# A two-part transformer block on one core: the split of the next batch's shift moved ahead of the token store, its load ahead of the stack, row and key loads, and the zero rows taken out

## The chip, the cores and the metric

The kernel runs on one core of one Trainium2 chip. The metric is the time of one execution on the device in microseconds (us). The kernel before was executed three times on the chip: 641.44, 649.53 and 644.13 us, median 644.13 us. Lower is better. Differences of under 2% count as no difference that can be told.

## The reference: what is computed

The inputs are `x` and `ctx_2048`, 16 batches of 128 rows by 512 features in fp32, two gates, and a mixture of 8 experts (`wg` 512x8, `W` 8x512x512, `b` 8x512).

```python
x = x + jnp.tanh(g_xattn[0]) * _L0_xattn_ref(_layernorm(x), ctx_2048, ctx_2048)
x = x + jnp.tanh(g_ffn[0]) * _L0_ffn_ref(_layernorm(x), wg, W, b)
# _L0_xattn_ref(q, k, v): 8 heads of 16 features over the 128 rows
qk = jnp.einsum('bdm,bdn->bmn', qh, kh) * scale      # 512 x 512 a head
ret = jnp.einsum('bmn,bcn->bcm', softmax(qk), vh)
# _L0_ffn_ref(x, wg, W, b): the one expert with the largest logit
idx = jnp.argmax(softmax(xt @ wg)); out = gate * (W[idx] @ xt + b[idx])
```

Here the 512 features of a row are the positions that attend to each other, and a head is 16 of the 128 rows. So a batch has 8 score matrices of 512x512, each with a contraction of only 16. The softmax subtracts the maximum of each of the 512 positions of a head, which the kernel calls the shift.

## The kernel before, in words

**Numbers in three parts.** To get fp32 accuracy from bf16 matmuls, GpSimd and ScalarE split q and k of a batch into three bf16 parts each (high, middle, low) and GpSimd stores them in DRAM (`parts_dram`, 768 KB a batch, L471). SyncE then loads them back stacked on the partitions: six terms of 16 rows are 96 rows (`KS`). `load_stack(B, g)` loads one half (g is 0 or 1, four heads each) of one batch: for q three copies of the high part, two of the middle and one of the low part (L329, each a broadcast of one source), for k the matching parts (L333), 192, 128 and 64 KB for each of the two. Rows 96 to 127 of a stack are padding: the three rows 96 to 98 (`KS` to `KS + NP`) of the k stack hold ones, those of the q stack hold the three bf16 parts of the shift, the others are zero. There are two stacks for even and odd batches (`B.p`).

**Two passes over the scores.** First the maxima: 32 matmuls of a batch write 128x512 scores into `ps_ring` (`scores_for_max`, L1099), two buffers, and VectorE takes the negated maximum of each (L756). After four of the eight heads PE transposes the maxima (L1105), VectorE copies them into `shift` (`take_maxima`), GpSimd splits them into three bf16 rows (`split_maxima`, L495 to L503) and SyncE copies these into the q stack (`load_shift`, L343, three small DMAs). Then the scores again, transposed and with the shift added by the matmul (`scores`, L1115, contraction over all 128 rows), exponentials on ScalarE (L672), and the product with the values and with ones (L1130). Because the maxima matmul also contracts over 128 rows, the shift rows of the q stack must be zero while it runs: `load_stack` ends with a seventh DMA that copies three rows of zeros there (L337).

**Rounds.** The kernel is written as 16 rounds of `emit(B, ...)` on each engine. Rounds 0 and 1 and 12 to 15 are straight code, rounds 2 to 11 are a hardware loop of two rounds in the body. In round B, PE works on the scores of batch B and between them on the maxima of batch B+1; the routing of batch B-2 and the split of q and k of batch B+3 lie in it too. The order on every engine is the order of the code, and engines meet at semaphores. On PE a round begins with the wait for `shift_in[0]` and `scores(B, 0, 0)`; directly behind stands the first maxima matmul of batch B+1, which waits for `stack_in[B.p][0]`, that is for all DMAs of `load_stack(B+1, 0)`.

**SyncE in round B**, in order: one slice of the expert weights, `load_shift(B, 1)`, the record of batch B-2, the residual input of batch B-1 (`load_residual`), `load_stack(B+2, 0)`, `load_rows_keys(B+4)` (x and k, 256 KB each), `load_shift(B+1, 0)`, `load_stack(B+2, 1)` and `load_values(B+2)`. `load_stack(B+2, 0)` waits until half of the scores of round B are done, `load_shift(B+1, 0)` until GpSimd's split of that shift (`shift_ready`), `load_stack(B+2, 1)` until all scores of round B are done. All these DMAs are on one queue.

**GpSimd in round B** ends the LayerNorm of x after attention (`rstd2`, L435 to L441), stores the token numbers of batch B-2 by an indirect DMA (`store_tokens`, L517 to L525), splits the shift (`split_maxima(B+1, 0)`), and makes and stores the low parts of batch B+3 (`lows`, L469 and L471).

After round 15 come 23 slots of the experts, to which the change does nothing.

Of the kernel before, what the change touches and what calls it, by code (L numbers as in the profile page):

```python
# [112 lines left out]
def build(nc, x_rows, x_perm, k_perm, v_t, w_t, wg_t, bias, g_attn, g_ffn, out):  # L113
    ctx = ExitStack()
    with ctx:
# [25 lines left out]
        slot_iota = sb("slot_iota", [128, 1])  # L141
        zeros = sb("zeros", [NP, NJ * DM], BF16)
        none_i = sb("none_i", [128, 128], I32)
# [122 lines left out]

        STACK_CONSTS, VALUE_CONSTS = 3, 4
        DVE_CONSTS = 17
        POOL_CONSTS = 13
# [28 lines left out]
        def _(sp):  # L298
# [20 lines left out]
            def load_stack(B, g):  # L319
# [12 lines left out]
                for first, n in ((0, 3), (3, 2), (5, 1)):  # L332
                    sp.dma_start(k_stack[first * DH:(first + n) * DH, B.p, g].rearrange("p j m -> p (j m)"),  # L333
                                 mine[1, g, 0:n].rearrange("t c m -> (t c) m")).then_inc(stack_in[B.p][g], 16)
                if B.known(0) and g == 0:
                    sp.wait_ge(pads_in, 16)
                sp.dma_start(q_stack[KS:KS + NP, B.p, g].rearrange("p j m -> p (j m)"),  # L337
                             zeros[:]).then_inc(stack_in[B.p][g], 16)

# [38 lines left out]
            def emit(B, prev, prev2, nxt, prep):  # L378
                load_weights(B)
                load_shift(B, 1)  # L380
                if B.known(NB - 1):
                    sp.wait_ge(scores_ready, 2 * STEPS * (NB - 1))
                    sp.dma_start(bias_sb.rearrange("p e n -> p (e n)"), bias.partition_broadcast(128)).then_inc(bias_in, 16)
                if prev2:
                    store_record(B.plus(-2))
                stack = not isinstance(B.b, int) or B.b + 2 < NB
                load_residual(B)
                if stack:
                    load_stack(B.plus(2), 0)
                if not isinstance(B.b, int) or B.b + 4 < NB:  # L390
                    load_rows_keys(B.plus(4))
                if nxt:
                    load_shift(B.plus(1), 0)
                if stack:
                    load_stack(B.plus(2), 1)
                    load_values(B.plus(2))
# [7 lines left out]
        def _(pool):  # L404
# [165 lines left out]
            def emit(B, prev, prev2, nxt, prep):  # L570
# [10 lines left out]
                if prev:  # L581
                    rstd2(B.plus(-1))
                if prev2 and not B.known(NB - 1):
                    store_tokens(B.plus(-2))
                if B.known(NB - 1):
# [3 lines left out]
                    for r in range(NREC):  # L589
                        gather(r, r)  # L590
                if nxt:
                    split_maxima(B.plus(1), 0)
                if prep:
# [134 lines left out]
        def _(dve):  # L728
# [3 lines left out]
                           lambda: nc.vector.memset(stacks[KS:KS + NP, 0, 1].rearrange("p g j m -> p (g j m)"), 1.0),  # L732
                           lambda: nc.vector.memset(zeros[:], 0.0),
                           lambda: nc.vector.memset(v_ones[:].rearrange("p a c g j d -> p (a c g j d)"), 1.0)]
# [356 lines left out]
        def _(pe):  # L1091
            def scores_for_max(B, u, n, k, chunks=range(NC)):

                g, j = divmod(k, NJ)
                if j == 0 and 0 in chunks:
                    pe.wait_ge(stack_in[B.p][g], B.i * (16 * 7) + 16 * 7)
                for c in chunks:
                    wait(pe, ring_free, u.free(n + c))
                    nc.tensor.matmul(ps_ring[:, u.slot(n + c)], q_stack[0:KA, B.p, g, j, c * 128:(c + 1) * 128],  # L1099
                                     k_stack[0:KA, B.p, g, j], start=True, stop=True).then_inc(ring_full, 1)  # L1100

# [6 lines left out]
            def scores(B, k, jp):  # L1108

                g, c = divmod(k, NC)  # L1110
                if c == 0 and jp == 0:
                    pe.wait_ge(shift_in[g], B.b * 48 + 48)
                wait(pe, exp_done, B.b * (2 * STEPS) + (2 * k + jp - 1))
                for j in (2 * jp, 2 * jp + 1):
# [201 lines left out]
```

## Time and profile before

| | us |
|---|---|
| median of 3 executions | 644.13 (641.44 to 649.53) |
| span of the profiled execution | 645.9 |
| first scores matmul of round 0 | at 57.91 |
| first scores matmul of round 2 | at 116.02 |
| first scores matmul of round 12 | at 413.33 |

Of the profiled execution the span is all that is reported; what lies around it is not given apart. The span is 1.8 us over the median of the three executions.

PE is busy 83% of the span, VectorE 73%, ScalarE 55%, GpSimd 50%. SyncE's DMA queue moves 62 MB, GpSimd's 25 MB. Times in a row of the trace are microseconds from the start of the span; a row of the chain of waits names what the end of the program waited for in turn; in a row of a stretch the numbers behind each engine are its busy time. In the text, S is the start of a round, the moment at which PE begins `scores(B, 0, 0)`: 326.07 for the round shown, 355.30 for the next.

### The profile page before, as it was taken

To read this page: it belongs to the slowest core of one execution; us is meant where nothing else is said; L and a number is where in the kernel's file an instruction comes from. 1 tells how busy PE (TensorE), PEld (TensorE's weight loads), DVE (VectorE), ACT (ScalarE), POOL (GpSimd) and SP (SyncE) were. 2 spreads that over 40 slices of the span, in tenths; PEclk is the share of its full clock that TensorE was granted. 3 is DMA by queue.
4 is the path that set the end of the run, shared out by engine and by line. 5 is a ranking of instruction groups with operands and counts; after the bars stand their busy time and mean duration, and the time that the engine had idled before them with its cause. 6 is when DMAs were issued, how large, how long until landed. Compare 5 with 4: busy or idle time off the path is not lost.

```text
span 645.9 us, 10904 instructions
## 1 busy us (share of the span) xinstructions
PE 533.8 (83%) x2584; PEld 179.0 (28%) x2585; DVE 469.3 (73%) x1017; ACT 352.5 (55%) x457; POOL 325.5 (50%) x574
## 2 busy tenths in 40 slices
PE   0077989798978989999988899889999776889994
PEld 0011222222222323323222322323233133444441
DVE  5387888696878979898988989798987636323332
ACT  2112867575766677686766677686666822111110
POOL 5431536282737556474736557474434436343541
PEclk9999999798999999999999999999999978999998
DMA  4734445364647574846657575835462645543320
GB/s 131 189 105 154 116 134 148 102 151 130 131 150 179 148 171 127 195 136 159 141 142 180 145 167 146 184 113 148 104 141 42 179 132 177 117 144 96 102 79 5
DMA packets 35290, 87.80 MB, mean 136 GB/s; under 512 B 10281, under 2 KB 10430, under 8 KB 35104
## 3 DMA queue, kind: packets, MB, share of 16 engines
q1 hardware_dynamic: 26208, 62.27, 39.3%
q0 software_dynamic: 9056, 25.23, 12.1%
q8 instruction: 11, 0.18, 0.1%
q14 instruction: 15, 0.12, 0.1%
HBM read 64.56 MB, written 27.11 MB: 142 GB/s over the span
## 4 chain that ended last, share of the span: by engine, by line
PE 31%; DMA 18%; DVE 17%; issue 11%; POOL 9%; SPq 3%; ACT 1%; POOLq 0%; DVEq 0%
DMA stacks<-shift_parts 13%; DVE neg_max L756 11%; PE ps_scores L1238 10%; PE ps_pv L1130 7%; PE ps_ring L1099 6%; PE ps_scores L1115 4%; DMA table_dram<-token_i,dest_i 2%; SPq L343 2%; DMA prep<-recs_dram,token_cols 2%; PE ps_pv L1147 2%; POOL table_dram L523 2%; POOL prep L463 2%; DVE den L794 1%; ACT probs L672 1%; PE ps_scores L1225 1%
## 5 line engine op out<-in xcount | busy, mean ns | idle before, releaser
L756 DVE TENSOR_REDUCE neg_max<-ps_ring 128x1 f32<-128x512 f32 x512 | 335.4, 680 | 76.1 <-PE ps_ring L1099 74.1
L672 ACT ACTIVATE probs<-ps_scores 128x1024 f32<-128x1024 f32 x256 | 249.2, 1022 | 112.0 <-PE ps_scores L1115 110.8
L1099 PE MATMUL ps_ring<-stacks 128*128 128x512 bf16 x512 | 201.0, 403 | 55.3 <-DMA stacks<-zeros 30.7
L1115 PE MATMUL ps_scores<-stacks 128*128 128x512 bf16 x512 | 156.1, 388 | 20.2 <-DMA stacks<-shift_parts 19.2
L1130 PE MATMUL ps_pv<-probs,v_ones 128*32 128x512 f32 x1024 | 138.2, 612 | 0.0
L1099 PEld LDWEIGHTS ps_ring<-stacks 128*128 128x128 bf16 x512 | 49.6, 97 | 240.6 <-DVE neg_max L756 191.0
L1238 PE MATMUL ps_scores<-w_sb,probs 128*128 x184 | 87.2, 619 | 3.3 <-DVE v_ones L927 1.3
L435 POOL TENSOR_SCALAR rs<-mv 128x1 f32<-128x1 f32 x32 | 6.1, 189 | 131.7 <-DVE mv L772 89.4
L1115 PEld LDWEIGHTS ps_scores<-stacks 128*128 128x128 bf16 x512 | 48.1, 101 | 65.4 <-issue 25.2
L710 ACT COPY probs<-ps_scores 128x512 f32<-128x512 f32 x23 | 13.4, 587 | 82.2 <-PE ps_scores L1225 82.2
L927 DVE TENSOR_TENSOR v_ones<-ps_scores,stacks 128x512 f32<-128x512 f32 x23 | 15.9, 692 | 57.6 <-PE ps_scores L1238 55.2
L1238 PEld LDWEIGHTS ps_scores<-w_sb,probs 128*128 128x128 f32 x184 | 34.4, 197 | 40.5 <-issue 40.4
L556 POOL DMA_INDIRECT out<-stacks,token_cols x23 | 23.5, 1023 | 43.3 <-DVE stacks L931 40.7
L463 POOL TENSOR_TENSOR prep<-prep 128x512 f32<-128x512 f32 x32 | 36.4, 1156 | 3.8 <-ACT prep L644 3.8
L469 POOL TENSOR_TENSOR prep<-prep 128x512 bf16<-128x512 f32 x32 | 36.2, 1149 | 0.0
L649 ACT CAST prep<-prep 128x512 bf16<-128x512 f32 x32 | 19.7, 618 | 25.2 <-POOL prep L463 25.2
L644 ACT CAST prep<-prep 128x512 bf16<-128x512 f32 x32 | 18.4, 619 | 24.0 <-DMA prep<-k_perm 17.5
L782 DVE STREAM_TRANSPOSE den_turned<-ps_pv 128x512 f32<-128x512 f32 x32 | 22.4, 699 | 11.0 <-PE ps_pv L1130 8.0
L484 POOL TENSOR_TENSOR num<-num,den 128x512 f32<-128x512 f32 x15 | 19.0, 1270 | 22.0 <-DVE den L794 19.5
L534 POOL COPY recip_turned<-recip 128x256 f32<-128x256 f32 x32 | 12.6, 393 | 33.8 <-DVE recip L788 33.8
L1130 PEld LDWEIGHTS ps_pv<-probs,v_ones 128*32 128x32 f32 x1024 | 20.3, 108 | 32.7 <-issue 19.7
L523 POOL DMA_INDIRECT table_dram<-token_i,dest_i x16 | 18.1, 1129 | 12.7 <-DVE neg_max L756 10.3
(138 smaller groups left out, 481.1 us busy)
## 6 DMA issues: line engine op xcount, KB each, us to landing
parts_dram<-prep POOLq DMA_DIRECT2D x16, 768.0 KB, 7.1
stacks<-parts_dram SPq DMA_DIRECT2D x64, 192.0 KB
recs_dram<-rec SPq DMA_DIRECT2D x16, 514.0 KB, 3.9
stacks<-parts_dram SPq DMA_DIRECT2D x64, 128.0 KB
w_sb<-w_t SPq DMA_DIRECT2D x16, 512.0 KB, 9.4
prep<-x_perm SPq DMA_DIRECT2D x16, 256.0 KB, 5.2
prep<-k_perm SPq DMA_DIRECT2D x16, 256.0 KB, 8.3
v_in<-v_t SPq DMA_DIRECT2D x16, 256.0 KB, 8.9
```

The lines of the kernel that those rows point to most:

```text
L463: nc.gpsimd.tensor_tensor(resid[:, s], src[:], parts[:, s, 0], ALU.subtract).then_inc(rest_ready, 1)
L469: nc.gpsimd.tensor_tensor(parts[:, s, 2], resid[:, s], parts[:, s, 1], ALU.subtract).then_inc(low_ready, 1)
L523: pool.indirect_dma_start(table_dram, bass.IndirectOffsetOnAxis(ap=dest_i[:, 0:1], axis=0), token_i[:], None).then_inc(table_out, 16)
L556: pool.indirect_dma_start(out, bass.IndirectOffsetOnAxis(ap=token_cols[:, s:s + 1], axis=0), y_out[r], None, bounds_check=NT - 1, oob_is_e ...
L649: nc.scalar.copy(parts[:, s, 1], resid[:, s]).then_inc(mid_cast, 1)
L672: nc.scalar.activation(probs[:, k % 2, 2 * jp:2 * jp + 2], ps_scores[:, jp], ACT.Exp).then_inc(exp_done, 1)
L756: nc.vector.tensor_reduce(neg_max[:, g, j, c:c + 1], ps_ring[:, u.slot(n)], AX.X, ALU.max, negate=True).then_inc(ring_free, 1)
L782: nc.vector.transpose(den_turned[:, g], ps_pv[:, g]).then_inc((low_turned, high_turned)[g], 1)
L1099: nc.tensor.matmul(ps_ring[:, u.slot(n + c)], q_stack[0:KA, B.p, g, j, c * 128:(c + 1) * 128], k_stack[0:KA, B.p, g, j], start=True, stop= ...
L1115: last = nc.tensor.matmul(ps_scores[:, jp, j % 2], k_stack[0:KA, B.p, g, j, c * 128:(c + 1) * 128], q_stack[0:KA, B.p, g, j], start=True, ...
L1130: last = nc.tensor.matmul(ps_pv[32 * j:32 * j + 32, g], v_ones[:, B.p, c, g, j], probs[:, k % 2, j], start=c == 0, stop=c == NC - 1)
L1238: last = nc.tensor.matmul(ps_y[:, r % 2], f_xt[:, r % 2, c], w_sb[:, c, bass.ds(e, 1)].rearrange("p o n -> p (o n)"), start=c == 0, stop=c ...
```

## The change

It has three parts. On GpSimd `split_maxima(B+1, 0)` moves ahead of `store_tokens(B-2)`. On SyncE `load_shift(B+1, 0)` moves ahead of `load_stack(B+2, 0)` and `load_rows_keys(B+4)`. And the maxima matmul contracts over 96 rows (`KS`) in place of 128, so that the DMA of the zero rows, its source buffer and that buffer's memset go; `load_stack` now issues six DMAs, and PE's wait counts six. The wait for the padding of the odd stacks (`pads_in`), which SyncE held ahead of the first zeros DMA, is now on PE ahead of the scores of batches 0 and 1.

```diff
@@ load_stack (SyncE) @@
                     sp.dma_start(k_stack[first * DH:(first + n) * DH, B.p, g].rearrange("p j m -> p (j m)"),
                                  mine[1, g, 0:n].rearrange("t c m -> (t c) m")).then_inc(stack_in[B.p][g], 16)
-                if B.known(0) and g == 0:
-                    sp.wait_ge(pads_in, 16)
-                sp.dma_start(q_stack[KS:KS + NP, B.p, g].rearrange("p j m -> p (j m)"),
-                             zeros[:]).then_inc(stack_in[B.p][g], 16)
@@ emit (SyncE) @@
                 load_residual(B)
+                if nxt:
+                    load_shift(B.plus(1), 0)
                 if stack:
                     load_stack(B.plus(2), 0)
                 if not isinstance(B.b, int) or B.b + 4 < NB:
                     load_rows_keys(B.plus(4))
-                if nxt:
-                    load_shift(B.plus(1), 0)
@@ emit (GpSimd) @@
                 if prev:
                     rstd2(B.plus(-1))
+                if nxt:
+                    split_maxima(B.plus(1), 0)
                 if prev2 and not B.known(NB - 1):
                     store_tokens(B.plus(-2))
...
-                if nxt:
-                    split_maxima(B.plus(1), 0)
                 if prep:
                     lows(B.plus(3))
@@ constants (VectorE) @@
-                           lambda: nc.vector.memset(zeros[:], 0.0),
@@ scores_for_max, scores (PE) @@
-                    pe.wait_ge(stack_in[B.p][g], B.i * (16 * 7) + 16 * 7)
+                    pe.wait_ge(stack_in[B.p][g], B.i * (16 * 6) + 16 * 6)
...
-                    nc.tensor.matmul(ps_ring[:, u.slot(n + c)], q_stack[0:KA, B.p, g, j, c * 128:(c + 1) * 128],
-                                     k_stack[0:KA, B.p, g, j], start=True, stop=True).then_inc(ring_full, 1)
+                    nc.tensor.matmul(ps_ring[:, u.slot(n + c)], q_stack[0:KS, B.p, g, j, c * 128:(c + 1) * 128],
+                                     k_stack[0:KS, B.p, g, j], start=True, stop=True).then_inc(ring_full, 1)
...
                     pe.wait_ge(shift_in[g], B.b * 48 + 48)
+                    if B.known(0) or B.known(1):
+                        pe.wait_ge(pads_in, 16)
```

**SyncE, in the middle of a round of the loop, before** (the program of the queue; `stacks<-shift_parts` is the shift load, `stacks<-parts_dram` the stack load, ISA and REGISTER_ALU rows are waits and register work):

```order
L317 DMA x_in<-x_rows 128x512
...
L329 DMA stacks<-parts_dram 48x1x2048
L329 ISA
L329 DMA stacks<-parts_dram 32x1x2048
...
L337 DMA stacks<-zeros 3x2048
L80 ISA
L303 ISA
L303 DMA prep<-x_perm 128x512
L304 DMA prep<-k_perm 128x512
L341 ISA
L343 DMA stacks<-shift_parts 1x16x128 x3
```

and now:

```order
L316 DMA x_in<-x_rows 128x512
L336 ISA
L338 DMA stacks<-shift_parts 1x16x128 x3
L80 ISA
L80 REGISTER_ALU
L328 ISA
L328 DMA stacks<-parts_dram 48x1x2048
...
L332 DMA stacks<-parts_dram 16x2048
L80 ISA
L302 ISA
L302 DMA prep<-x_perm 128x512
L303 DMA prep<-k_perm 128x512
```

The shift load with its wait stands directly behind the residual input, and the stack, row and key loads stand behind it; the zeros DMA is gone.

**GpSimd, between the statistics of LayerNorm 2 and the low parts, before:**

```order
L441 TENSOR_TENSOR rs<-rs,minus 128x1
L80 REGISTER_ALU
L517 CAST dest_i<-dest_f 128x1
L518 CAST token_i<-token_f 128x1
L74 REGISTER_ALU
L523 DMA table_dram<-token_i,dest_i 16384x1
L525 TENSOR_SCALAR token_f<-token_f 128x1
L493 REGISTER_ALU
L495 CAST shift_parts<-shift 16x128
...
L503 TENSOR_TENSOR shift_parts<-shift_rest,shift_parts 16x128
```

and now:

```order
L436 TENSOR_TENSOR rs<-rs,minus 128x1
L488 REGISTER_ALU
L490 CAST shift_parts<-shift 16x128
...
L498 TENSOR_TENSOR shift_parts<-shift_rest,shift_parts 16x128
L80 REGISTER_ALU
L512 CAST dest_i<-dest_f 128x1
L513 CAST token_i<-token_f 128x1
L74 REGISTER_ALU
L518 DMA table_dram<-token_i,dest_i 16384x1
```

The four instructions of the split have changed places with the token store; their number is the same.

## Rows read from the trace of the kernel before

**Rows 1.** The waits, longest first: engine, line, releaser, us in total, times, longest.

```profile
PE ps_scores L1115 <- DMA stacks<-shift_parts: 19.2, 12, 3.1
```

**Rows 2.** Stretches: us, busy us of each engine, PEclk, DMA share, GB/s.

```profile
57.91:85.80 27.89, 25.96 (x122) 7.20 (x123) 22.52 (x38) 19.16 (x22) 10.41 (x20) 1.00 0.37 104
85.80:116.02 30.22, 25.18 (x134) 7.22 (x135) 24.17 (x43) 20.70 (x25) 15.54 (x28) 0.98 0.60 149
116.02:413.33 297.31, 264.14 (x1440) 83.23 (x1441) 253.88 (x560) 209.61 (x270) 173.02 (x320) 0.98 0.60 150
413.33:441.97 28.64, 26.01 (x145) 8.26 (x145) 25.46 (x55) 20.58 (x27) 17.20 (x32) 1.00 0.47 140
441.97:469.41 27.44, 25.88 (x145) 8.16 (x144) 24.45 (x54) 18.53 (x23) 10.76 (x23) 1.00 0.51 117
116.02:146.10 30.08, 28.42 (x144) 8.71 (x144) 24.70 (x55) 20.66 (x27) 17.35 (x32) 0.90 0.52 125
148.96:177.94 28.98, 27.36 (x144) 8.50 (x144) 24.68 (x55) 20.64 (x27) 17.30 (x32) 0.94 0.55 124
326.07:354.09 28.02, 26.04 (x144) 8.24 (x144) 24.69 (x55) 20.54 (x27) 17.28 (x32) 1.00 0.62 157
```

**Rows 3.** The chain of waits at the end of the round shown: start, us, what.

```profile
348.79 6.39 DMA stacks<-shift_parts
```

**Rows 4.** PE by time: start, us, instruction, count, idle before it and releaser.

```profile
341.71 0.59 PE L1115 MATMUL ps_scores<-stacks 128*128 128x512 bf16 x2
...
355.30 0.60 PE L1115 MATMUL ps_scores<-stacks 128*128 128x512 bf16 x2 [1.21 <-DMA stacks<-shift_parts]
355.73 0.38 PE L1099 MATMUL ps_ring<-stacks 128*128 128x512 bf16 x1
```

**Rows 5.** SyncE's queue by time, in the same round.

```profile
339.87 0.35 SPq L317 DMA_DIRECT2D x_in<-x_rows  x1
340.68 2.40 SPq L329 DMA_DIRECT2D stacks<-parts_dram  x3
343.29 1.25 SPq L333 DMA_DIRECT2D stacks<-parts_dram  x3
344.60 0.73 SPq L337 DMA_DIRECT2D stacks<-zeros  x1
...
346.13 0.37 SPq L304 DMA_DIRECT2D prep<-k_perm  x1
347.53 1.85 SPq L343 DMA_DIRECT2D stacks<-shift_parts  x3
351.75 2.59 SPq L329 DMA_DIRECT2D stacks<-parts_dram  x3
```

**Rows 6.** GpSimd by time, in the same round, and the same line in round 0.

```profile
75.19 0.42 POOL L503 TENSOR_TENSOR shift_parts<-shift_rest,shift_parts 16x128 bf16<-16x128 f32 x1
...
343.14 0.19 POOL L441 TENSOR_TENSOR rs<-rs,minus 128x1 f32<-128x1 f32 x1
...
345.81 0.28 POOL L495 CAST shift_parts<-shift 16x128 bf16<-16x128 f32 x1
...
347.08 0.42 POOL L503 TENSOR_TENSOR shift_parts<-shift_rest,shift_parts 16x128 bf16<-16x128 f32 x1
```

**Rows 7.** DMA issues from 340 to 360 us: KB each, us from issue to landing.

```profile
x_in<-x_rows SPq DMA_DIRECT2D x1, 256.0 KB, 3.3
prep<-k_perm SPq DMA_DIRECT2D x1, 256.0 KB, 8.5
```

**Rows 8.** Stretches of one us, columns as in rows 2.

```profile
351.00:352.00 1.00, 0.86 (x5) 0.24 (x3) 1.00 (x3) 0.99 (x2) 1.00 (x3) 1.00 0.19 65
352.00:353.00 1.00, 1.00 (x9) 0.16 (x8) 1.00 (x3) 0.95 (x2) 0.31 (x2) 1.00 1.02 365
```

**Rows 9.** The start: SyncE's first stack load, and PE's first maxima matmul.

```profile
16.71 2.42 SPq L329 DMA_DIRECT2D stacks<-parts_dram  x3
...
30.69 1.01 PE L1099 MATMUL ps_ring<-stacks 128*128 128x512 bf16 x2 [30.69 <-DMA stacks<-zeros]
```

More of the change, by code:

```diff
@@ L141, in build @@
         slot_iota = sb("slot_iota", [128, 1])
-        zeros = sb("zeros", [NP, NJ * DM], BF16)
         none_i = sb("none_i", [128, 128], I32)
@@ L265, in build @@
         y_stored = [sem(f"y_stored{r}") for r in range(NREC)]
-        STACK_CONSTS, VALUE_CONSTS = 3, 4
-        DVE_CONSTS = 17
+        STACK_CONSTS, VALUE_CONSTS = 2, 3
+        DVE_CONSTS = 16
         POOL_CONSTS = 13
```

## The prediction, as it stood before the result

> **What bounds the kernel now.** I read the waits first, then stretches of rounds, the chain of waits, and the queues of the round that starts at S = 326.07.
>
> The waits say what the change aims at: PE stands 19.2 us in 12 waits, at most 3.1 us each, at the first scores of a round, for the shift load [rows 1]. The stretches put it in scale. Ten rounds from 116.02 to 413.33 take 297.3 us, 29.7 each, while an undisturbed one is through its work in 28.0 us and waits for the rest [rows 2]. PE is busy 26.0 of those 28.0 us, VectorE 24.7. So nothing shorter than 28.0 us a round can come of this change, about 17 us in all. Rounds 2 and 3, which follow waits of about 3 us, take 30.1 and 29.0 us of work at granted clocks of 0.90 and 0.94, a mix of the 2.4 and the 1.2 GHz level [rows 2].
>
> The chain ends a round with the last of the three shift DMAs, issued at 348.79 and landed 6.4 us later, at 355.2; PE's scores begin at 355.30 and the first maxima matmul of the batch after next follows 0.43 us behind [rows 3, 4]. The reader should look at who is ahead of that DMA: on the same queue the stack load from 340.68, the zeros, and x and k; GpSimd is done with the split only at 347.5, because the token store lies before it [rows 5, 6].
>
> The decisive question is what becomes of the stack load, which the change puts behind the shift. PE needs it 0.43 us after the shift, at the same place of its program. Its own landing isn't shown, so I read it from its neighbours. k, issued at 346.13 behind it, takes 8.5 us and lands at 354.6, while x_in with little ahead of it takes 3.3 us for the same 256 KB [rows 7]. And from 351 to 352 the 16 DMA engines are busy for a share of 0.19, about three engines, although k and the shift are still out [rows 8]. A few engines have a tail of stack packets that the others have finished.
>
> **The change part by part.**
>
> *Split ahead of the token store.* GpSimd ends the LayerNorm statistics at 343.33 (343.14 + 0.19) and the split takes 1.69 us (345.81 to 347.50) [rows 6]. It will be done at 345.0, that is S + 18.95, 2.5 us earlier. The token store slips by 1.7 us; its result is wanted a round later, and the low parts behind both end where they did. Cost nothing.
>
> *Shift load first.* SyncE has issued x_in at 340.2 and now waits for the split until 345.0. The three shift DMAs take 1.85 us to issue [rows 5]. Last issue S + 20.2; with 3.3 us, as for x_in [rows 7], or even with 6.4 us [rows 3], they land by S + 26.6, before PE is ready at S + 28.0. The wait of rows 1 goes: up to -17 us in the loop by itself.
>
> *The stack load behind it.* It was issued from 340.68, S + 14.6; now from 345.0 + 0.05 + 1.85 + 0.3 (SyncE's steps between loads in the loop) = 347.2, S + 21.15: 6.5 us later. How long from the first issue to the landing?
> - At least 7.2 us: its issues take 3.9 us (340.68 to 344.54) [rows 5], and the last then needs the 3.3 us of x_in [rows 7].
> - At most 14.0 us: the first stack load of the kernel is issued from 16.71, and PE starts on it at 30.69 [rows 9], with 512 KB of padding ahead of it.
> - Nearest is k behind it: landed 354.6, so 13.9 us after 340.68 with the 512 KB of x and k in it. At the 365 GB/s of a full stretch [rows 8] these take 1.4 us; that leaves 12.5 for the stack load.
> I take 13.0: the parts store of GpSimd, 768 KB from about 352 on [rows 8], lay only at the end of the stack load before and now falls inside it. The range and the rivals keep 7.2 and 14.0.
>
> The Trainium skill (DMA: Bandwidth & Descriptors, Rules for kernel authors) says that a leading broadcast of c copies confines a DMA to at most c engines. By it the three-copy and two-copy loads of q put 16 packets of 4 KB each on the same first engines, and the tail is what it should be; the share of 0.19 in rows 8 agrees. Had all 16 engines shared the load, the sum would be that of the first rival below.
>
> *The next round.* The stack lands at S + 21.15 + 13.0 = S + 34.15. The maxima matmul starts 0.14 later, and a round counts from 0.43 before it: a round lasts 33.9 us in place of 29.7. PE stands about 5.6 us in it.
>
> *What is behind the stack load.* The key load is issued at about S + 25.5 in place of S + 20.1 [rows 5] and lands behind the stack, about 1.5 us into the next round's maxima; it is wanted 3 us in. The second half of the stack (351.75, S + 25.7) was waiting for the scores and moves by a few tenths. No cost.
>
> *Zero rows.* Each of 28 stack loads in the rounds loses an issue of 0.73 us [rows 5], on a queue whose engine waits. At the start four of them lie on the way to the first shift: gain between 0 and 2.9 us; I take 0.8, for they are 12 KB against 768. The matmul with 96 rows has no row in this trace; its columns stay 512, and between nothing and a quarter of its 0.38 us [rows 4] I take nothing, since VectorE's maxima stand behind each. The memset of the zeros lies before the first parts have landed.
>
> *The clock.* Waits of about 3 us were followed by 2.05 and 0.96 us of extra work time in rounds 2 and 3 (30.08 and 28.98 against 28.02) [rows 2], and by none in the round after. Mean 1.0 us. The new standstill is longer and comes every round: 1.0 us for each of 13 rounds is 13; between 0 and 2.05 each.
>
> **The sum**, without the clock:
>
> | rounds | before [rows 2] | now | difference |
> |---|---|---|---|
> | 0 (split done at 75.61, S + 17.7 [rows 6]) | 27.9 | 17.7 + 1.95 + 13.0 - 0.29 = 32.4 | +4.5 |
> | 1, as 0 | 30.2 | 32.4 | +2.2 |
> | 2 to 11 | 297.3 | 10 x 33.9 = 339 | +41.7 |
> | 12, straight code | 28.6 | 33.6 | +5.0 |
> | 13, without the parts store | 27.4 | 33.0 | +5.6 |
>
> That is +59.0, less 0.8 at the start, plus 13 for the clock: +71.2. On the span of 645.9 us this is 717; the median of the runs is 1.8 us lower, so **715 us**. The ends: a landing of 12.5 us and no cost of the clock give 14 x 0.5 less, +51, 695 us; 14.0 us and 2.05 us a round give +14 + 13.7, +99, 743 us.
>
> **The rivals.**
> - *The stack load spreads over all engines and is in time* (faster). Landing 7.2 us after the first issue, at S + 28.35, just when the maxima matmul wants it (28.0 + 0.43). Then 17 us of waits go, 3 us of slow clock behind them and 0.8 at the start: 623 us. For it: 365 GB/s are reached at times [rows 8], and 768 KB at that rate take 2.1 us. Against it: k's 8.5 us and the start [rows 7, 9]. It decides from a landing under 29.73 - 21.15 - 0.14 + 0.43 = 8.9 us, where the round is as long as now. The Trainium skill (DMA: Bandwidth & Descriptors, Bandwidth) has 1 MB in 6.15 us over 128 partitions, of which an estimate for 768 KB would be 4.6 us, on this side too. Chance 0.09.
> - *In between*: 9 to 12 us, if traffic of x_in, records and parts had stretched the tail before. At 10.5 a round is 31.4: (10.5 - 13.0) x 14 = -35, some 680 us with part of the clock. Chance 0.13, of it 0.05 within 2%.
> - *The other shift becomes late as well* (slower still). Its three DMAs stand behind the second stack half. With the first landed 0.3 us into the round, x and k 1.4, the second half some 10 and values and weights 2, it lands at S + 13.5 to 14; PE wants it at 341.71, S + 15.6 [rows 4]. Slack 2 us. If the tails are longer by 3 us, each round gains one more: 13 to 30 us, 745 us. Chance 0.08.
> - That the change doesn't do what it says is excluded by the order of the two queues.
>
> My forecast has 0.70. The range takes in its ends and most of the case in between: 674 to 743 us. Within 2% is 631 to 657 us, about what a measurement of this kernel can tell from no change. Faster 0.08, same 0.06, slower 0.86.
>
> **What the profile after would show.** The waits of PE for the shift gone, and in their place, at the first maxima matmul of a round, one of about 5 us for the stack load in each of rounds 1 to 14. SyncE's stack load first issued at S + 21. The shift's three DMAs landing in 2 to 4 us. Rounds of 33 to 36 us, with a granted clock under 1 in the stretch behind most of these waits. The split done at S + 19, the token store behind it. I am wrong if the stack load lands within 9 us of its first issue; then the round falls to its 28.0 us.

## The result: 755 us, slower by 17.5%

The changed kernel takes **755.1 us** (median of 4 runs, 753.6 to 758.7), the kernel before beside it 646.1. The ratio is **1.175** (95% interval 1.167 to 1.183); ratios in this document compare executions in the chip's faster state alone, so they aren't the quotients of the medians. I had forecast 715 us in a range of 674 to 743: the sign and the order of waits came out, the size didn't, and the time lies 12 us over the range.

The page of the kernel after: span, busy us of PE and VectorE, then the granted clock of TensorE and the DMA share in 40 equal slices.

```profile
span 753.2 us, 10831 instructions
PE 561.6 (75%) x2544; PEld 187.2 (25%) x2585; DVE 469.1 (62%) x1016; ACT 353.9 (47%) x457; POOL 325.0 (43%) x574
PEclk9999897789787788988888899999998998899998
DMA  4642617161718162626161627261514255454230
```

The DMA engines now work in bursts, and the clock falls in the same rhythm. Its mean is 0.892, where it was 0.975.

The waits after: engine, line, releaser, us in total, times, longest.

```profile
PE ps_ring L1093 <- DMA stacks<-parts_dram: 132.8, 15, 30.9
PEld ps_ring L1093 <- DMA stacks<-parts_dram: 28.0, 4, 8.3
```

The wait for the shift [rows 1] is gone from this list. The wait for the stack load took its place: 15 waits of the matmuls, of which the longest is the start of the kernel, as in [rows 9], and 4 of the weight loads. They are those of the first maxima matmul of a round. PE by time shows three of them, with the idle time in brackets:

```profile
355.17 0.60 PE L1093 MATMUL ps_ring<-stacks 96*128 96x512 bf16 x1 [6.64 <-DMA stacks<-parts_dram]
...
392.98 0.61 PE L1093 MATMUL ps_ring<-stacks 96*128 96x512 bf16 x1 [6.25 <-DMA stacks<-parts_dram]
...
433.51 0.60 PE L1093 MATMUL ps_ring<-stacks 96*128 96x512 bf16 x1 [9.11 <-DMA stacks<-parts_dram]
```

From 91.13 to 579.12 there are 14 such rows, each of 5.2 to 9.5 us, and a round between two of them lasts 37.5 us.

GpSimd's rows of the round that starts at 355.17, the counterpart of [rows 6], and SyncE's queue, that of [rows 5]:

```profile
375.47 0.28 POOL L490 CAST shift_parts<-shift 16x128 bf16<-16x128 f32 x1
...
376.74 0.42 POOL L498 TENSOR_TENSOR shift_parts<-shift_rest,shift_parts 16x128 bf16<-16x128 f32 x1
...
378.23 1.11 POOL L518 DMA_INDIRECT table_dram<-token_i,dest_i  x1 [0.81 <-POOL token_i L513]
...
382.56 0.94 POOL L466 DMA_DIRECT2D parts_dram<-prep  x1 [0.68 <-POOL prep L464]
```

```profile
377.19 1.79 SPq L338 DMA_DIRECT2D stacks<-shift_parts  x3
379.46 2.28 SPq L328 DMA_DIRECT2D stacks<-parts_dram  x3
...
383.97 0.38 SPq L303 DMA_DIRECT2D prep<-k_perm  x1
384.70 2.17 SPq L328 DMA_DIRECT2D stacks<-parts_dram  x3
```

Everything that has to come first stands in this order: split, shift, stack. The second half of the stack is issued 5.2 us behind the first half; it was 11.1 us behind [rows 5]. The token store, which stood 3.7 us behind the first issue of the stack load, now stands 1.2 us ahead of it, and the parts store stands 3.1 us behind it in place of 9.7. Before, in the round of [rows 5] with its stack load at 340.68, the two stood here:

```profile
344.42 1.12 POOL L523 DMA_INDIRECT table_dram<-token_i,dest_i  x1 [0.79 <-DVE neg_max L756]
...
350.42 0.95 POOL L471 DMA_DIRECT2D parts_dram<-prep  x1 [0.68 <-POOL prep L469]
```

The chain of waits hangs on the stack: the load's last DMA, issued at 382.82, takes 10.0 us, and PE goes on 0.12 us later.

```profile
382.82 10.04 DMA stacks<-parts_dram
```

Landings in the window of 376 to 392 us (columns of [rows 7], the last being us from issue to landing):

```profile
parts_dram<-prep POOLq DMA_DIRECT2D x1, 768.0 KB, 9.9
...
prep<-k_perm SPq DMA_DIRECT2D x1, 256.0 KB, 10.7
stacks<-shift_parts SPq DMA_DIRECT2D x3, 4.0 KB, 1.7
```

Stretches, columns as in [rows 2]: ten rounds, one round, and pieces of that round from its beginning.

```profile
127.18:507.75 380.57, 288.44 (x1416) 91.42 (x1442) 254.31 (x560) 210.93 (x270) 172.58 (x320) 0.85 0.43 118
355.17:392.98 37.81, 30.04 (x142) 9.67 (x145) 25.44 (x56) 21.15 (x27) 17.27 (x32) 0.82 0.36 106
351.00:355.00 4.00, 0.00 (x0) 0.00 (x0) 0.00 (x0) 0.00 (x0) 0.00 (x0) 0.54 1.06 282
355.00:361.00 6.00, 5.83 (x21) 2.32 (x22) 3.63 (x8) 1.02 (x1) 0.00 (x0) 0.50 0.27 103
361.00:365.00 4.00, 4.00 (x14) 1.48 (x18) 2.22 (x7) 2.23 (x3) 2.85 (x9) 0.50 0.09 34
365.00:369.00 4.00, 3.80 (x26) 0.98 (x20) 3.63 (x11) 3.43 (x7) 1.27 (x1) 1.00 0.02 3
```

Ten rounds take 380.6 us against 297.3, with the same numbers of VectorE and GpSimd instructions. In one round PE is busy 30.0 us where an undisturbed one of [rows 2] had 26.0. Behind the wait of 6.64 us PE works at 1.2 GHz (0.50) for ten microseconds, from 355 to 365, before the clock is back. And in the four us before PE goes on, from 351 to 355, the DMA share is 1.06: the last packets of the stack load don't go out on otherwise idle engines here, as they did before [rows 8], but beside other loads. All but 0.05 of that share are packets of SyncE's queue; those of GpSimd's, the parts store, take a share of 0.3 to 0.7 from 347 to 351.

### The profile page after: what moved, and what is told of

It reads as the page before. It is cut to its first block, busy times and chain, and to the rows that moved or that the text cites. A ratio compares the mean times of both kernels' runs of the same rounds, so it can differ in the third digit from the quotient of the medians.

```text
span 753.2 us, 10831 instructions
## 1 busy us (share of the span) xinstructions
PE 561.6 (75%) x2544; PEld 187.2 (25%) x2585; DVE 469.1 (62%) x1016; ACT 353.9 (47%) x457; POOL 325.0 (43%) x574
## 4 chain that ended last, share of the span: by engine, by line
DMA 30%; PE 28%; DVE 13%; issue 10%; SPq 10%; POOL 7%; DVEq 0%; POOLq 0%; ACT 0%
DMA stacks<-parts_dram 21%; DVE neg_max L750 8%; PE ps_ring L1093 7%; PE ps_pv L1126 7%; PE ps_scores L1234 6%; SPq L328 4%; PE ps_scores L1111 4%; SPq L338 3%; DMA prep<-recs_dram,token_cols 3%; DMA prep<-k_perm 2%; SPq L332 2%; PE ps_pv L1143 2%; DMA table_dram<-token_i,dest_i 2%; POOL prep L458 2%; DVE den L788 1%
## 5 line engine op out<-in xcount | busy, mean ns | idle before, releaser
L1093 PE MATMUL ps_ring<-stacks 96*128 96x512 bf16 x512 | 213.0, 430 | 153.4 <-DMA stacks<-parts_dram 132.8
L1126 PE MATMUL ps_pv<-probs,v_ones 128*32 128x512 f32 x1024 | 149.1, 657 | 0.0
L1093 PEld LDWEIGHTS ps_ring<-stacks 96*128 96x128 bf16 x512 | 50.2, 98 | 354.2 <-DVE neg_max L750 195.9
L1234 PE MATMUL ps_scores<-w_sb,probs 128*128 x184 | 85.3, 607 | 2.5 <-issue 1.4
L1111 PEld LDWEIGHTS ps_scores<-stacks 128*128 128x128 bf16 x512 | 51.7, 106 | 47.5 <-issue 9.8
L705 ACT COPY probs<-ps_scores 128x512 f32<-128x512 f32 x23 | 13.4, 586 | 79.5 <-PE ps_scores L1221 79.5
L551 POOL DMA_INDIRECT out<-stacks,token_cols x23 | 23.5, 1023 | 40.1 <-DVE stacks L925 37.6
L464 POOL TENSOR_TENSOR prep<-prep 128x512 bf16<-128x512 f32 x32 | 36.2, 1149 | 0.0
L479 POOL TENSOR_TENSOR num<-num,den 128x512 f32<-128x512 f32 x15 | 19.0, 1269 | 27.6 <-DVE den L788 25.0
L776 DVE STREAM_TRANSPOSE den_turned<-ps_pv 128x512 f32<-128x512 f32 x32 | 22.3, 698 | 11.0 <-PE ps_pv L1126 8.0
## 6 DMA issues: line engine op xcount, KB each, us to landing
w_sb<-w_t SPq DMA_DIRECT2D x16, 512.0 KB, 13.1
```

Of the source, the lines that this page charges most:

```text
L464: nc.gpsimd.tensor_tensor(parts[:, s, 2], resid[:, s], parts[:, s, 1], ALU.subtract).then_inc(low_ready, 1)
L551: pool.indirect_dma_start(out, bass.IndirectOffsetOnAxis(ap=token_cols[:, s:s + 1], axis=0), y_out[r], None, bounds_check=NT - 1, oob_is_e ...
L776: nc.vector.transpose(den_turned[:, g], ps_pv[:, g]).then_inc((low_turned, high_turned)[g], 1)
L1093: nc.tensor.matmul(ps_ring[:, u.slot(n + c)], q_stack[0:KS, B.p, g, j, c * 128:(c + 1) * 128], k_stack[0:KS, B.p, g, j], start=True, stop= ...
L1111: last = nc.tensor.matmul(ps_scores[:, jp, j % 2], k_stack[0:KA, B.p, g, j, c * 128:(c + 1) * 128], q_stack[0:KA, B.p, g, j], start=True, ...
L1126: last = nc.tensor.matmul(ps_pv[32 * j:32 * j + 32, g], v_ones[:, B.p, c, g, j], probs[:, k % 2, j], start=c == 0, stop=c == NC - 1)
```

## The experiments

All ratios are to the kernel before, run on the same chip, with their 95% interval. S is the start of a round, as before. "Landing" is the time from the first issue of a round's stack load to the last increment of its semaphore, read from the trace as a mean over rounds. It is 14.6 us in the kernel after (12.9 to 16.7, 14 loads) and was 12.8 before (12.0 to 14.1). The length of a round is the mean of rounds 2 to 11, from first scores to first scores: 29.7 us before, 38.0 after.

### The parts alone

**e1: the change with SyncE's old order.** What is left is the split ahead of the token store, and no zeros.

```diff
                 load_residual(B)
-                if nxt:
-                    load_shift(B.plus(1), 0)
                 if stack:
                     load_stack(B.plus(2), 0)
                 if not isinstance(B.b, int) or B.b + 4 < NB:
                     load_rows_keys(B.plus(4))
+                if nxt:
+                    load_shift(B.plus(1), 0)
```

> The changed kernel with SyncE's order of before (stack, rows and keys, then the shift); the split ahead of the token store and the missing zero rows stay. Theory A (a stack load leaves a tail on a few DMA engines, and the loss is that it starts 6.5 us later): the stack is issued at S + 14.6 again and is in time; the shift is ready earlier but lands behind the same tail, at about S + 28.6 in place of 29.1. Time 635 to 646 us, within 2% of before. Theory B (the loss is in the 96-row matmul or in the late token store): 750 us, as the changed kernel. Theory C (the shift's landing follows its issue, not the tail): 625 us.

Measured 669.7 us, 1.027 (1.020 to 1.035). My theory missed: the order accounts for most of the loss, but the rest should have been a small gain and is a loss. The waits of e1:

```profile
PE ps_scores L1111 <- DMA stacks<-shift_parts: 39.2, 12, 5.9
```

It is twice that of [rows 1], although the split is done earlier. The stack landed 14.1 us after its issue here, and the shift stands behind it: its last DMA lands 10.5 us after its issue (mean of ten rounds), where it took 6.5 before. So it comes at S + 32.7 in place of S + 29.6, although it is issued 0.8 us earlier, and a round takes 32.9 us.

**e2: SyncE's new order alone.**

```diff
                 load_residual(B)
+                if nxt:
+                    load_shift(B.plus(1), 0)
                 if stack:
...
-                if nxt:
-                    load_shift(B.plus(1), 0)
```

> The kernel before with SyncE's order alone changed (shift, stack, rows and keys); the split stays behind the token store, the zero rows stay. Theory A: the stack waits for a split that is ready 2.5 us later than in the changed kernel, in rounds 2 to 13: 755 + 12 x 2.5 = 785 us. Theory B (the other two parts carry the loss): 650 us. If only the combination costs: under 755 us.

Measured 783.8 us, 1.214 (1.204 to 1.224), as worked out beforehand: the split is 2.5 us later than in the kernel after, and a round takes 39.6 us. A wait of its PE by time:

```profile
370.50 0.61 PE L1099 MATMUL ps_ring<-stacks 128*128 128x512 bf16 x1 [10.58 <-DMA stacks<-zeros]
```

So the load order costs the bulk of the loss, 137 us alone and 85 us with the earlier split (e1 to the kernel after).

**e6: only the zero rows gone.** The stack load has six DMAs and the maxima matmuls 96 rows.

```diff
-                sp.dma_start(q_stack[KS:KS + NP, B.p, g].rearrange("p j m -> p (j m)"),
-                             zeros[:]).then_inc(stack_in[B.p][g], 16)
...
-                    nc.tensor.matmul(ps_ring[:, u.slot(n + c)], q_stack[0:KA, B.p, g, j, c * 128:(c + 1) * 128],
+                    nc.tensor.matmul(ps_ring[:, u.slot(n + c)], q_stack[0:KS, B.p, g, j, c * 128:(c + 1) * 128],
```

> The kernel before with the third part of the change alone: 96 rows in the maxima matmul and no zeros DMA; split and shift load where they were. It takes apart the 22 us that e1 is slower than before, against its expectation. Theory E (the loss of e1 comes of GpSimd's new order: the token store now runs into the tail of the stack load and the parts store): 636 to 646 us, as before or a little better. Theory F (it comes of the missing zeros or of the 96-row matmul): 665 us or more.

Measured 651.9 us, 1.008 (1.005 to 1.011), over the 636 to 646 that I expected: nothing gained, a trace lost, and not the loss that would have explained e1. The group of its maxima matmuls:

```profile
L1093 PE MATMUL ps_ring<-stacks 96*128 96x512 bf16 x512 | 200.7, 403 | 55.7 <-DMA stacks<-parts_dram 31.0 <-DVE neg_max L750 12.8 <-ACT probs L667 1.8
```

512 matmuls of 96 rows take 403 ns in the mean. The kernel before has 403 ns for 128 rows as well:

```profile
L1099 PE MATMUL ps_ring<-stacks 128*128 128x512 bf16 x512 | 201.0, 403 | 55.3 <-DMA stacks<-zeros 30.7 <-DVE neg_max L756 12.9 <-ACT probs L672 1.6
```

**e11: only the split moved ahead of the token store.** The mirror of e2, on GpSimd.

```diff
                     rstd2(B.plus(-1))
+                if nxt:
+                    split_maxima(B.plus(1), 0)
                 if prev2 and not B.known(NB - 1):
                     store_tokens(B.plus(-2))
...
-                if nxt:
-                    split_maxima(B.plus(1), 0)
```

> The kernel before with the second part of the change alone: the split of the shift ahead of the token store on GpSimd; SyncE's order and the zeros as before. e6 (zeros alone) was 0.8% slower than before, e1 (zeros and split) 2.7%. Theory E (the moved token store carries e1's loss): 660 to 675 us, although the split is ready 2.5 us earlier. Rival (the two parts only cost together): 640 to 648 us.

Measured 674.4 us, 1.041 (1.031 to 1.051), inside what was expected. This is e1's loss by itself: its wait for the shift is 43.4 us in 12, at most 6.5, and the stack lands after 14.4 us (up to 18.2). With the old order the earlier split can gain little anyway: SyncE reaches the shift at 346.13 + 0.37 = 346.5, 1.0 us before the split's end at 347.5 [rows 5, 6]. What it moves is the token store, from 3.7 to 5.3 us behind the first issue of the stack load. The shift's last DMA lands 9.8 us after its issue, nearly as late as in e1.

### The landing of the stack

**e3: the kernel after with the q loads cut into DMAs of 16 rows**, nine per stack load instead of six, none with a broadcast of copies in front.

```diff
-                    sp.dma_start(q_stack[first * DH:(first + n) * DH, B.p, g].rearrange("p j m -> p (j m)"),
-                                 mine[0, g, t].unsqueeze(0).to_broadcast([n, DH, NJ * DM])
-                                 ).then_inc(stack_in[B.p][g], 16)
+                    for i in range(first, first + n):
+                        sp.dma_start(q_stack[i * DH:(i + 1) * DH, B.p, g].rearrange("p j m -> p (j m)"),
+                                     mine[0, g, t]).then_inc(stack_in[B.p][g], 16)
...
-                    pe.wait_ge(stack_in[B.p][g], B.i * (16 * 6) + 16 * 6)
+                    pe.wait_ge(stack_in[B.p][g], B.i * (16 * 9) + 16 * 9)
```

> The changed kernel with the three-copy and the two-copy load of q written as three and two loads of 16 rows each: nine DMAs of 16, 32 or 48 rows in place of six, the same bytes. Theory A: each spreads over all engines, the tail goes, the stack lands 6 to 8 us after its first issue in place of 14.6, at S + 28 to 30, and rounds take 28 to 30 us: 620 to 655 us. Theory D (the landing is long because of the total traffic, x, k, parts and the other half included, not because of a few engines): the landing stays over 12 us and the time over 730 us.

Measured 666.9 us, 1.029 (1.023 to 1.035). The mechanism holds: 88 us of the 109 go. The size is short of what I expected (620 to 655 us), since the landing fell to 9.7 us (8.2 to 12.1), and not to 6 to 8. Its waits:

```profile
PE ps_ring L1093 <- DMA stacks<-parts_dram: 57.7, 15, 24.3
```

**e4: the same loads with SyncE's old order** (e1 and e3 together).

> The q loads as in the run with nine DMAs, but SyncE's order of before (e1's kernel with nine DMAs). Theory A: stack issued early and no tail in front of the shift: it lands within 3 us of its issue, PE waits neither for the shift nor for the stack, rounds of 28.0 us, full clock: 620 to 630 us, the best so far. Theory D: as e1, 640 us.

Measured 613.9 us, 0.947 (0.942 to 0.952): better than expected, and the fastest of all. Its waits and, from a window of 300 to 330 us, the landing of two loads:

```profile
PE ps_ring L1093 <- DMA stacks<-parts_dram: 25.3, 1, 25.3
PE ps_scores L1111 <- DMA stacks<-shift_parts: 2.1, 3, 0.9
...
prep<-k_perm SPq DMA_DIRECT2D x1, 256.0 KB, 3.7
stacks<-shift_parts SPq DMA_DIRECT2D x6, 4.0 KB, 2.3
```

The stack lands after 7.2 us and k behind it after 3.7 instead of 8.5 [rows 7]. The row of the shift is the median of six DMAs; the last of three, which PE waits for, took 6.4 us before [rows 3] and takes 6.3 here (mean of ten rounds), not the 3 that I expected. With the tail, in e1, it took 10.5. Against the kernel before it is issued 1.8 us earlier (S + 21.3 against S + 23.1); so it lands at S + 27.6, is hardly waited for any more, and a round takes 28.1 us, about the length of its work. PE's first maxima matmul also comes 5.4 us earlier, since the first load at the start lands sooner, and the first scores 9.1 us earlier (48.80 against 57.91).

**e7: the kernel before with the q loads cut up**, nothing else.

> The kernel before, with nothing of the change, and the three-copy and two-copy loads of q as DMAs of 16 rows (ten DMAs a stack load in place of seven). Theory A: the tail alone was what made the shift late before; it lands within 6 us of its issue and before PE wants it, rounds of 28.0 us, and the start is shorter: 612 to 622 us, within 1% of e4, so the change's own parts give nothing on top. Rival: the change's parts are needed as well: 630 us or more.

Measured 617.4 us, 0.957 (0.953 to 0.962), as expected. The waits for the shift are down to this:

```profile
PE ps_scores L1115 <- DMA stacks<-shift_parts: 4.9, 7, 1.8
```

So most of the shift wait that the change attacks goes with the tail of the stack load alone, with the old order on both queues: the shift's last DMA lands after 5.4 us instead of 6.5, at S + 28.1 instead of S + 29.6, and a round takes 28.4 us. That is 13 us over rounds 2 to 11; another 9 of the 30 us lie at the start, where the first scores begin at 48.51. The stack lands after 9.6 us here (7.2 to 11.9), not after e4's 7.2. And the new order loses 53 us even with the short tail (e3 against e4).

Why does the tail exist? The Trainium skill (DMA: Bandwidth & Descriptors, Rules for kernel authors) says that a leading broadcast of c copies confines a DMA to at most c engines, and these runs agree: without the broadcasts the load lands after 7.2 us instead of 14.1 (e4 against e1). An estimate by that rule is that of the 192 packets of 4 KB of a stack half two engines get 39 each (16 and 16 of the broadcasts, 7 of the rest), where an even spread would give each 12. The traces here don't name the engine of a packet.

**e8: the change with the shift between the stack and rows and keys.**

```diff
                 load_residual(B)
-                if nxt:
-                    load_shift(B.plus(1), 0)
                 if stack:
                     load_stack(B.plus(2), 0)
+                if nxt:
+                    load_shift(B.plus(1), 0)
                 if not isinstance(B.b, int) or B.b + 4 < NB:
```

> The changed kernel with the shift load between the stack load and the rows and keys, six DMAs a stack load as in the change. Theory A: the stack is issued at S + 14.6 and lands in time, the shift stands behind its tail but no longer behind rows and keys, and lands about 1 us earlier than in e1: 10 to 14 us under e1's 670, 655 to 660 us. If rows and keys ahead of the shift cost nothing: 670 us.

Measured 636.7 us, 0.983 (0.976 to 0.991). I expected 655 to 660 and missed on the good side, though against the kernel before the gain is under 2%: the shift wait is 9.8 us in 8, the stack lands after 13.1 us, and a round takes 29.0 us. I had charged the shift with the whole tail in front of it. But SyncE, waiting for the split, holds x and k back as well, and these no longer join the stack on the engines. Against e1 the shift's last DMA is issued 1.9 us earlier (S + 20.4 against S + 22.3) and lands 2.1 us sooner after that (8.4 against 10.5). That the second part comes of the held x and k is argued, not shown.

**e10: the kernel after, with SyncE holding x, k and the second half until the first half has landed.**

```diff
                     load_stack(B.plus(2), 0)
+                    sp.wait_ge(stack_in[B.p][0], B.plus(2).i * (16 * 6) + 16 * 6)
```

> The changed kernel, with SyncE waiting until load_stack(B+2, 0) has landed before it issues rows, keys and the second half. The other side of e9. Theory H: the landing falls from 14.6 to about 13 us. Theory G: it stays at 14 to 15 us. In time the landing gained and the rows and keys that now come late at the next round's start may cancel: 735 to 775 us.

Measured 739.0 us (two runs), 1.139 (1.125 to 1.152). The landing is 13.4 us on the mean, and a round takes 37.0 us. Its queue and PE:

```profile
330.68 2.27 SPq L328 DMA_DIRECT2D stacks<-parts_dram  x3
333.27 1.26 SPq L332 DMA_DIRECT2D stacks<-parts_dram  x3
344.37 0.35 SPq L302 DMA_DIRECT2D prep<-x_perm  x1
```

```profile
344.21 0.61 PE L1094 MATMUL ps_ring<-stacks 96*128 96x512 bf16 x1 [6.25 <-DMA stacks<-parts_dram]
```

With nothing of SyncE's behind it the load of this round too still takes from 330.7 to 344.1, 13.4 us. The traffic behind accounts for about 1.2 of the 14.6 us. The rest is the load's own tail, the token store and the parts store. The tail can be seen in this run: from 340 to 342 and from 342 to 344 the DMA share is 0.16 and 0.08, one to three engines of 16, while PE waits for the stack.

### The clock

**e5: the kernel after, with 24 matmuls on constants between the scores and the first maxima matmul**, so that PE works where it waited.

```diff
+                    if nxt and k == 0 and B.b is not None and not B.known(0):
+                        wait(pe, ring_free, u.free(n))
+                        for _ in range(24):
+                            nc.tensor.matmul(ps_ring[:, u.slot(n)], ones_bf[:], filler[:], start=True, stop=True)
```

> The changed kernel, and in rounds 1 to 15, once PE has done the first scores and before it waits for the stack load, 24 matmuls of constants (128x128 by 128x512, bf16) into the free buffer of ps_ring, which the true matmul then overwrites: some 5 us of work inside a wait of 6 to 8 us. It leaves the waits and the loads as they are. Theory A' (of the 755 us the clock is a larger part than the 13 us of my sum: after each wait the granted clock is at the 1.2 GHz level for a while, and the next shift is issued 20.7 us after the first maxima matmul on the mean of 13 rounds, where an undisturbed round has 18.4): clock near 1.0 in the rounds, the time 20 to 32 us lower, 723 to 735 us. If the clock costs only what my sum had: 742 us. If it costs nothing: 755 us or more.

Measured 745.7 us, 1.150 (1.140 to 1.161), with runs from 738 to 758: less gained than the 20 to 32 us that I expected. The clock rose from 0.892 to 0.958. PE by time at the place:

```profile
372.51 5.34 PE L1185 MATMUL ps_ring<-filler,ones_bf 128*128 128x512 bf16 x24
378.01 0.39 PE L1095 MATMUL ps_ring<-stacks 96*128 96x512 bf16 x1 [0.16 <-DMA stacks<-parts_dram]
```

The filling takes 5.34 us, the wait behind it shrinks to 0.16, and the first maxima matmul takes 0.39 us instead of 0.60. From a landing to the next first issue it is 21.8 us instead of 22.9, and a round between two first maxima matmuls 36.2 instead of 37.5. In five rounds of the loop, this one among them, the granted clock is 1.00 between these two points, and they lie 20.9 to 21.0 us apart, where I had 20.86. The 9 us of gain are a lower bound of what the clock costs, because in seven of 13 rounds it still fell.

### The token store

**e9: the kernel after without the token store.** A plain DMA of 512 bytes to a scratch tensor stands in its place.

```diff
-                pool.indirect_dma_start(table_dram, bass.IndirectOffsetOnAxis(ap=dest_i[:, 0:1], axis=0),
-                                        token_i[:], None).then_inc(table_out, 16)
+                pool.dma_start(scratch_dram, none_i[0:1, :]).then_inc(table_out, 16)
```

> The changed kernel with the token store left out: in place of the indirect DMA of 128 four-byte writes GpSimd issues one plain DMA of 512 bytes to a scratch buffer at the same place. The routing table stays empty, so the expert stage after round 15 moves no rows, and its time isn't to be compared; the rounds are. It asks why a stack load lands 14.6 us after its first issue in the changed kernel (mean of 14) where 12.8 was read before. Theory G (the token store, issued 1.2 us ahead of the stack load, holds up all 16 DMA engines for 2 to 4 us when they next read): landings of 12.5 to 13.5 us, none over 14.5, rounds 1 to 2 us shorter than 37.5. Theory H (x, k and the second half crowd them): 14 to 15 us as now.

Its 735.6 us can't be set against the kernel before, since the end has no rows to move; its rounds can. The landing is 13.6 us (at most 14.5) instead of 14.6, about as expected, but rounds 2 to 11 take 37.6 us instead of 38.0, less than the 1 to 2 us expected. The clock took the rest back: from a landing to the next first issue TensorE is at 1.2 GHz for 8.5 us on the mean instead of 6.5, and the way takes 23.7 us instead of 22.9.

**e12: e1 without the token store**, the same edit.

> e1's kernel with the token store left out in the way of e9; the expert stage moves no rows, so rounds are to be compared. Theory G: with the store gone the tails are the 12.7 us of before and the rounds 28.5 to 29.5 us on the mean of rounds 2 to 11, where e1's are 32. If the split's place costs in another way (its own instructions, the shift's issue): 31 us or more.

Rounds 2 to 11 take 29.9 us, against 32.9 in e1 and 29.7 before. That is between the two expectations (28.5 to 29.5, or over 31) and nearer to the theory. The waits for the shift:

```profile
PE ps_scores L1111 <- DMA stacks<-shift_parts: 16.9, 9, 3.9
```

They were 39.2 us in e1. The landing of the stack fell from 14.1 to 12.1 us, that of the shift's last DMA from 10.5 to 8.1. So without the store e1's loss is all but gone, and by its likeness I take the same for e11. But the store's place alone isn't enough: e8 has it at the same place, 5.3 us behind the first issue of the stack, and loses nothing. In these runs it costs where x, k and then the shift stand behind a stack load with its tail. And no run took the store out of the kernel before, so what its place costs and what it costs anywhere aren't told apart.

One-us stretches of e1 behind the token store that is issued at 336.40 show what it does (columns as in [rows 2]; the share counts a packet's whole time where the packet starts):

```profile
343.00:344.00 1.00, 1.00 (x12) 0.40 (x5) 0.58 (x2) 0.33 (x1) 0.40 (x1) 1.00 2.55 311
344.00:345.00 1.00, 0.47 (x4) 0.08 (x2) 0.49 (x1) 0.59 (x1) 0.00 (x0) 1.00 0.14 49
345.00:346.00 1.00, 0.00 (x0) 0.00 (x0) 0.20 (x1) 0.00 (x0) 0.00 (x0) 1.00 0.55 53
```

The packets that start in the first of them last 2.55 us' worth of all 16 engines, and little starts in the two behind (49 and 53 GB/s), while loads are outstanding. PE is idle from 344.5 on, waiting for the shift.

## Why the prediction was right and wrong

**Direction: right.** The shift wait went, the stack wait took its place in rounds 1 to 14 at the first maxima matmul, and the split, the shift and the stack stand in the expected order. The shift's DMAs land in 1.7 us (forecast 2 to 4), and PE doesn't wait for them. The other shift isn't late; that rival is out. "The stack spreads over all engines" is out for the kernel as it stands, and e4 shows its 7.2 us to be the right price once the loads are cut up and start early (e3, with the new order, has 9.7).

**Where the 40 us are.** My sum was 717 us on the span, and it is 753.2: 36 us. The other 4 come of a slip: I took 1.8 us off the span to get the median, but an execution here lasts at least 1.6 us beyond its span (754.81 against 753.2), so the profiled one before was itself slower than the median. Thirteen rounds, from the first maxima matmul at 91.13 to that at 579.12, take 37.54 us each. The form that I used for rounds 2 to 11 gives 33.9 and 1.0 for the clock, 34.9. Of the 2.66 us between:
- **First issue to landing, the term that failed:** 14.59 us measured, 13.0 forecast, 1.6 us a round, 21 us in all. My upper end of 14.0 was itself too low. As a reading of the kernel before, where it is 12.8, the step was right; it failed by carrying that over to a place where the load's company is another. I named the parts store, and priced it by choosing 13.0 over 12.5. Two more things had moved closer: x, k and the second half stand right behind the load (e10: 1.2 us of landing), and the token store comes 1.2 us ahead of it (e9: 1.0 us of landing, but only 0.4 of a round). Each was measured with the other in place, so they need not add up.
- **The clock:** landing to next first issue is 22.93 us, forecast 20.86 and 1.0. That leaves 2.1 us of clock in place of 1.0, 14 us over 13 rounds. I took the mean of what two waits of 3 us had cost, with an upper end of 2.05; the waits of 5 to 9 us cost that end on the mean, 0.6 to 4.8 us each. That the term is the clock is shown: at 1.00 the way takes the 20.9 us that I had (e5), and in the kernel after it takes 21.4 to 22.5 us in eight rounds at a granted clock of 0.88 to 0.92, 24.2 to 24.4 in four at 0.80 and 25.7 in one at 0.75. It doesn't follow the length of the wait: 3.3 us at 1.2 GHz came behind the wait of 9.1 us at 433.51 and 9.9 behind that of 6.6 at 355.17. I should have put the standstill that I forecast, 5.6 us, beside the rows and seen that all of them had shorter ones.

These two make 35 of the 36 us. The rest is what is left of rounds 1, 12 and 13 and the start, which I priced some 3 us lower, and an end that is 2 us shorter.

**"The token store slips; cost nothing": wrong.** With the old order its move costs 4.1% (e11), while the split's lead over it gains at most the 1.0 us a round that SyncE had been waiting. I asked when the store's result is wanted. I didn't ask what the store does to the transfers around it, though the change moved it relative to every one of them. In the kernel after it is the smaller part of the miss, 1.0 us of landing and 0.4 of a round (e9), since the stack's order dominates.

**Zero rows: right within 1%.** Nothing was gained (e6, +0.8%), and the matmul's 403 ns don't depend on 96 or 128 rows.

**What stays open.** Why packets stall behind the indirect store, why in e1 in every round of the loop but in the kernel after in about half, and why that costs so little in e7 and e8, where it happens as often. Whether x's and k's later issue is what lets the shift land sooner in e8. And what of the landing in the kernel after is the parts store: no run moved it.

## What to carry to other kernels

When a small transfer is late behind a large one on the same queue, look first at why the large one takes so long: cutting its broadcasts into 16-row DMAs gave 4.3% with no order changed (e7), a third of it at the start of the kernel, while putting the small one first cost 17.5%, because the large one was wanted 0.4 us later at the same place. Price a moved load by its landing in its new company, not by the old one, and keep the end of the range beyond the nearest row when everything around it draws closer. And count the standstill twice: once for its length and once for the slow clock behind it.

## What the runs showed of the hardware, unexpected

- Behind an indirect store of 128 words of 4 bytes, 512 bytes in all, packets of other transfers can take 1.5 to 4.2 us each, where 19 of 20 take under 0.5 us. In e1 6 to 12 such packets start 6.4 to 7.7 us after the store's issue in each of rounds 2 to 11; in the kernel after 7 to 18 of them, from 2.8 us after it, in six of these rounds; in the kernel before groups of four and more in four. In the same rounds e9, without the store, has none and e12 a single one. Between the rounds of e1 and of e12 lie 3.0 us.
- A load of 768 KB in which five of six copies of q come by two broadcasts lands after 14.1 us (e1), 12.8 (before) and 14.6 (after); with the same bytes in 16-row DMAs it lands after 7.2 (e4), 9.6 (e7) and 9.7 (e3). What is behind it on the same queue is late too: k took 8.5 us before and 3.7 in e4, the last shift DMA of 4 KB 10.5 us in e1 and 6.3 in e4.
- After a standstill of 6.6 us TensorE ran at 1.2 GHz for ten more microseconds of full work, after one of 9.1 us for 3.3. Matmuls on constants in the gap kept it at 2.4 GHz in six of 13 rounds and gained 9 us of 755.
